# Local attention on row halves: scores and weighted values per head, on 64 rows and 32 columns of TensorE, in two parts

## The reference, cut to what matters

```
q, k, v = split(shift_tokens(x) @ Wqkv)            # to heads
q, k = rotate(l2norm(q) * q_scale), rotate(l2norm(k) * k_scale)
# every window of 32 queries sees the 64 keys of its own and the window before it
sim = einsum('bhwie,bhwje->bhwij', bq, bk2) * 8    # masked to a band
out = einsum('bhwij,bhwje->bhwie', softmax(sim), bv2)
x = out @ Wo + x
x = ffn_layer(shift_tokens(x)) + x                 # LayerNorm, W1, gelu gate, W2
```

## Time and profile before

| what | value |
|---|---|
| median of 3 runs | 6410.44 us (6407.3 to 6416.03) |
| the profiled execution | 6418.48 us, span 6416.7 us |
| PE, PEld busy | 5762.8 us (90%), 3834.2 us (60%) |
| DVE, ACT, POOL busy | 4902.8 us (76%), 3303.9 us (51%), 2795.0 us (44%) |
| L593 and L625, MATMUL | x12288 each, 274 ns each in the mean |
| mean granted clock of PE | 0.939 of full |
| HBM read, written | 36.20 MB, 1.05 MB |

### The profile page before, as it was taken

The page is one execution under the profiler, slowest core; times in us unless marked ns, Lnnn a source line. Parts: engine busy times, 40 slices in busy tenths (PEclk is TensorE's granted clock), DMA queues, the critical chain, the costliest instruction groups (busy, mean ns, idle before and its releaser), DMA issues. The chain is left out here.

```text
span 6416.7 us, 142352 instructions
## 1 busy us (share of the span) xinstructions
PE 5762.8 (90%) x47596; PEld 3834.2 (60%) x47596; DVE 4902.8 (76%) x9448; ACT 3303.9 (51%) x7050; POOL 2795.0 (44%) x3439
## 2 busy tenths in 40 slices
PE   4776999999999978988988998898699999999998
PEld 1334666666666644675566567457466666666665
DVE  5995776767676729998998999899577777677775
ACT  3334776777776732222222222223277777777775
POOL 1224666656666611222122123122266666666663
PEclk7998999999999988999999998999799999999998
DMA  0001222222222200000000000000022222222221
GB/s 16 0 0 53 67 74 71 67 66 67 73 64 73 65 22 0 1 1 1 0 1 1 1 1 1 1 1 1 23 68 73 65 74 64 75 68 70 68 67 41
DMA packets 163281, 247.28 MB, mean 39 GB/s; under 512 B 36980, under 2 KB 57392, under 8 KB 162486
## 3 DMA queue, kind: packets, MB, share of 16 engines
q1 hardware_dynamic: 162614, 238.71, 14.2%
HBM read 36.20 MB, written 1.05 MB: 6 GB/s over the span
## 5 line engine op out<-in xcount | busy, mean ns | idle before, releaser
L1428 PE MATMUL psum<-tk_kT,tk_qs 128*128 128x512 f32 (+3 forms) x4128 | 1255.7, 465 | 9.2 <-POOL tk_qs L1661 9.2
L1661 POOL TENSOR_TENSOR tk_qs<-tk_qT,tk_mix 128x1024 f32<-128x1024 f32 x258 | 495.7, 1924 | 1564.9 <-PE psum L1429 1441.8
L929 POOL TENSOR_TENSOR f_rope<-f_rope,f_t 128x1024 f32<-128x1024 f32 x384 | 905.5, 2358 | 476.7 <-DVE f_t L843 476.2
L1428 PEld LDWEIGHTS psum<-tk_kT,tk_qs 128*128 128x128 f32 x4128 | 757.0, 208 | 432.4 <-issue 290.2
L1618 DVE MAX8 tk_m<-tk_work 128x8 f32<-128x528 f32 (+3 forms) x1792 | 818.5, 496 | 2.2 <-issue 1.1
L942 POOL TENSOR_TENSOR f_rope<-f_rope,f_rn 128x1024 f32<-128x1024 f32 x384 | 730.5, 1902 | 59.9 <-POOL f_rn L921 4.4
L479 PE MATMUL psum<-f_wqkv,f_xs 128*128 128x512 f32 x1536 | 736.5, 602 | 16.7 <-DVE f_t L843 16.7
L1624 DVE MATCH_REPLACE8 tk_work<-tk_m,tk_work 128x400 f32<-128x400 f32 (+3 forms) x1536 | 744.0, 491 | 0.3
L848 DVE TENSOR_REDUCE f_ss<-f_sq 128x16 f32<-128x1024 f32 x384 | 466.0, 1213 | 339.3 <-ACT f_sq L710 334.6
L673 ACT ACTIVATE f_kT<-psum 64x512 f32<-64x512 f32 (+1 forms) x960 | 485.3, 525 | 82.5 <-PE psum L470 73.2
L1545 ACT ACTIVATE tk_o_tok<-psum,tk_rden 128x64 f32<-128x64 f32 (+1 forms) x256 | 80.0, 313 | 869.6 <-DVE tk_rden L1602 869.5
(11 more groups left out here) (235 smaller groups left out, 10226.4 us busy)
## 6 DMA issues: line engine op xcount, KB each, us to landing
f_v<-f_v_tok SPq DMA_DIRECT2D x1152, 128.0 KB, 2.4
f_v<-f_v_tok SPq DMA_DIRECT2D x768, 64.0 KB, 2.0
f_wqkv<-in_Wqkv SPq DMA_DIRECT2D x36, 512.0 KB, 5.2
f_wo<-in_Wo SPq DMA_DIRECT2D x12, 512.0 KB, 4.3
f_w<-in_W SPq DMA_DIRECT2D x12, 341.0 KB, 3.3
f_w<-in_W SPq DMA_DIRECT2D x24, 64.0 KB
tk_wkv<-in_Wkv SPq DMA_DIRECT2D x1, 1024.0 KB, 6.0
out<-y_tok SPq DMA_DIRECT2D x4, 256.0 KB, 2.5
```

What stands on the lines that cost most here:

```text
L929: pool.tensor_tensor(part, part, t2[:, half, :, :], ALU.add).then_inc(s[f"{name}_added"], 1)
L1428: pe.matmul(psum[:, j, 0:n], qs[:, j, c, :], kT[:, c, 0:n], start=(c == 0), stop=False, skip_group_check=True)
L1661: pool.tensor_tensor(qs[:, j, :, :], qT[:, :, P * t:P * (t + 1)], mix[:, :, heads(p, j)].to_broadcast([P, PAIRS, P]), ALU.mult).then_inc(s ...
```

## The change

Each head gets matmuls of its own on the 64 rows that hold it: 64 rows by 32 columns of weights, 64 moving columns. The zero blocks go: `kT` and `v2` lose the index `par`. The even heads' results go to bank 4, the odd heads' to bank 5, and VectorE reads and writes `o_tok` and `prob` by parity. `weigh` and `score` get an argument: part 0 makes pairs 0 to 3, part 1 pairs 4 to 7. `weigh(0)` stands ahead of `turn_keys` and `weigh(1)` behind it; `score(0)`, with the mask, stands behind `queries`, `score(1)` where `score` was. Part 0 waits only for the first bank's copies. ScalarE copies a bank's keys in one piece.

```diff
-        kT = sb("kT", [P, PAIRS, 2, WIN + 2 * P])
+        kT = sb("kT", [P, PAIRS, WIN + 2 * P])
-        v2 = sb("v2", [P, 2, WPT, 2, PAIRS, DH])
+        v2 = sb("v2", [P, 2, WPT, PAIRS, DH])
+        def by_parity(x):
+            return x.rearrange("p (c r) e -> p r c e", r=2)
...
-                            sp.dma_start(v2[r0:r0 + 2 * WIN, slot, w, par, :, :], v_tok[WIN * (w - 1):WIN * (w + 1), slot, par, :, :]).then_inc(v_in, 16)
+                            sp.dma_start(v2[r0:r0 + 2 * WIN, slot, w, :, :], v_tok[WIN * (w - 1):WIN * (w + 1), slot, par, :, :]).then_inc(v_in, 16)
...
-                    def weigh():
+                    def weigh(part):
                         if on(g, 2):
-                            for n in range(2):
-                                wait(pe, f"pt{n}_evac", through(g, 2))
-                            wait(pe, "sub_done", through(g, 2))
-                            pe.wait_ge(v_sem(j % 2), 1 + v_count(g - 2, j))
-                            for c in range(PAIRS):
+                            if part == 0:
+                                wait(pe, "sub_done", through(g, 2))
+                                pe.wait_ge(v_sem(j % 2), 1 + v_count(g - 2, j))
+                            wait_apart(pe, f"pt{part}_evac", through(g, 2))
+                            for c in range(4 * part, 4 * part + 4):
                                 for w in range(WPT):
-                                    last = pe.matmul(psum[WIN * w:WIN * (w + 1), 4 + c // 4, (c % 4) * P:(c % 4 + 1) * P],
-                                                     probT[:, c, WIN * w:WIN * (w + 1)], v2[:, j % 2, w, :, c, :], start=True, stop=True)
-                            last.then_inc(s["pv_done"], 1)
+                                    for par in range(2):
+                                        rows = slice(DH * par, DH * (par + 1))
+                                        last = pe.matmul(psum[WIN * w:WIN * (w + 1), 4 + par, c * DH:(c + 1) * DH],
+                                                         probT[rows, c, WIN * w:WIN * (w + 1)], v2[rows, j % 2, w, c, :], start=True, stop=True)
+                            if part:
+                                last.then_inc(s["pv_done"], 1)
...
-                    def score():
+                    def score(part):
                         if on(g, 1):
-                            for n in range(2):
-                                wait(pe, f"kt{n}_evac", through(g, 1))
-                                wait(pe, f"qt{n}_evac", through(g, 1))
-                            if on(g, 2):
-                                wait(pe, "on_done", through(g, 2))
                             sj = (j - 1) % 4
...
+                            wait(pe, f"kt{part}_evac", through(g, 1))
+                            if part == 0:
+                                if on(g, 2):
+                                    wait(pe, "on_done", through(g, 2))
+                                for par in range(2):
+                                    pe.matmul(psum[:, 4 + par, :], k.ident_bf[:, :], k.band[:, int(sj == 0), :, :].rearrange("p h w -> p (h w)"),
+                                              start=True, stop=False, skip_group_check=True)
+                            wait_apart(pe, f"qt{part}_evac", through(g, 1))
+                            for c in range(4 * part, 4 * part + 4):
...
+                                        last = pe.matmul(psum[WIN * w:WIN * (w + 1), 4 + par, c * 2 * WIN:(c + 1) * 2 * WIN],
+                                                         qT[rows, c, WIN * w:WIN * (w + 1)], kT[rows, c, t0:t0 + 2 * WIN],
+                                                         start=False, stop=True, skip_group_check=True)
...
+                    weigh(0)
                     turn_keys()
-                    weigh()
+                    weigh(1)
                     if f is not None and j == 2:
                         gated(1)
                     turn_queries()
                     queries()
+                    score(0)
                     if f is not None and j == 2:
                         gated(2)
-                        score()
+                        score(1)
                         output()
                     else:
                         output()
-                        score()
+                        score(1)
...
-                            for par in range(2):
-                                rows = slice(DH * par, DH * (par + 1))
-                                if sj == 1:
-                                    copy(kT[rows, 4 * n:4 * n + 4, par, 0:WIN], turned[rows, :, P - WIN:P])
-                                last = copy(kT[rows, 4 * n:4 * n + 4, par, slot:slot + P], turned[rows, :, :])
-                            last.then_inc(s[f"kt{n}_evac"], 1)
+                            if sj == 1:
+                                copy(kT[:, 4 * n:4 * n + 4, 0:WIN], turned[:, :, P - WIN:P])
+                            copy(kT[:, 4 * n:4 * n + 4, slot:slot + P], turned).then_inc(s[f"kt{n}_evac"], 1)
...
-                        dve.tensor_tensor(prob[:, :, :], sc_bank, top[:, :].unsqueeze(2).to_broadcast([P, H, 2 * WIN]), ALU.subtract).then_inc(s["sub_done"], 1)
+                        dve.tensor_tensor(by_parity(prob[:, :, :]), psum[:, 4:6, :].rearrange("p r (c w) -> p r c w", w=2 * WIN),
+                                          top[:, :].rearrange("p (r c) -> p r c", r=2).unsqueeze(3).to_broadcast([P, 2, PAIRS, 2 * WIN]),
+                                          ALU.subtract).then_inc(s["sub_done"], 1)
```

More of the change, by code:

```diff
@@ L426, in spread_v @@
                         r0 = DH * par
-                        sp.dma_start(v2[r0:r0 + WIN, slot, 0, par, :, :], v_tok[P - WIN:P, 1 - slot, par, :, :]).then_inc(v_in, 16)
-                        sp.dma_start(v2[r0 + WIN:r0 + 2 * WIN, slot, 0, par, :, :], v_tok[0:WIN, slot, par, :, :]).then_inc(v_in, 16)
+                        sp.dma_start(v2[r0:r0 + WIN, slot, 0, :, :], v_tok[P - WIN:P, 1 - slot, par, :, :]).then_inc(v_in, 16)
+                        sp.dma_start(v2[r0 + WIN:r0 + 2 * WIN, slot, 0, :, :], v_tok[0:WIN, slot, par, :, :]).then_inc(v_in, 16)
                         for w in range(1, WPT):
-                            sp.dma_start(v2[r0:r0 + 2 * WIN, slot, w, par, :, :], v_tok[WIN * (w - 1):WIN * (w + 1), slot, par, :, :]).then_inc(v_in, 16)
+                            sp.dma_start(v2[r0:r0 + 2 * WIN, slot, w, :, :], v_tok[WIN * (w - 1):WIN * (w + 1), slot, par, :, :]).then_inc(v_in, 16)
                 def layer(L):
@@ L609, in output @@
                             last.then_inc(s["wo_full"], 1)
-                    def score():
+                    def score(part):
                         if on(g, 1):
-                            for n in range(2):
-                                wait(pe, f"kt{n}_evac", through(g, 1))
-                                wait(pe, f"qt{n}_evac", through(g, 1))
-                            if on(g, 2):
-                                wait(pe, "on_done", through(g, 2))
-                            sj = (j - 1) % 4
-                            for half in range(2):
-                                pe.matmul(psum[:, 4 + half, :], k.ident_bf[:, :], k.band[:, int(sj == 0), :, :].rearrange("p h w -> p (h w)"),
-                                          start=True, stop=False, skip_group_check=True)
-                            for c in range(PAIRS):
+                            sj = (j - 1) % 4
+                            wait(pe, f"kt{part}_evac", through(g, 1))
[7 more added lines that the diff above has]
+                            for c in range(4 * part, 4 * part + 4):
@@ L623, in score @@
                                 for w in range(WPT):
                                     t0 = P * (sj % 2) + WIN * w
-                                    last = pe.matmul(psum[WIN * w:WIN * (w + 1), 4 + c // 4, (c % 4) * P:(c % 4 + 1) * P],
-                                                     qT[:, c, WIN * w:WIN * (w + 1)], kT[:, c, :, t0:t0 + 2 * WIN],
-                                                     start=False, stop=True, skip_group_check=True)
-                            last.then_inc(s["scores"], 1)
+                                    for par in range(2):
+                                        rows = slice(DH * par, DH * (par + 1))
+                                        last = pe.matmul(psum[WIN * w:WIN * (w + 1), 4 + par, c * 2 * WIN:(c + 1) * 2 * WIN],
+                                                         qT[rows, c, WIN * w:WIN * (w + 1)], kT[rows, c, t0:t0 + 2 * WIN],
+                                                         start=False, stop=True, skip_group_check=True)
@@ L630, in turn_output @@
+                            if part:
+                                last.then_inc(s["scores"], 1)
                     def turn_output():
@@ L815, in _ @@
             def _(dve):
-                dve.memset(kT[:, :, :, :], 0.0).then_inc(s["zeroed"], 1)
```

(7 more changed lines are left out.)

## The result

The changed kernel takes 6499.27 us in the median (6496.07 to 6502.99, 4 runs), beside 6409.9 for the kernel before in the same comparison: ratio 1.0138, 95% interval 1.0123 to 1.0153. It is slower by 1.4%; 6263 us had been forecast. No run of it came near the forecast range (6155 to 6397).

A forecast was written before the change was run, and what follows sets the result against it. TensorE's own work was taken to set the pace, with other limits close behind. Groups of four steps gave -151 us, memsets -10.8, jitter took back 14: -148 from 6418.5, less 8 for the profiled execution, 6263 us; range 6155 to 6397.

The forecast's parts named there:

- So issue is not what makes 27 ns today; the length of the moving rows is.: Matmul pricing: weight loads starting 7 ns apart were read as showing that moving-row length, not issue, sets 27 ns per record.
- Rival 3: All `weigh` and `score` matmuls: each costs 27 ns whatever its length, +3.86 us a step, ending at 7140; chance 5%.
- The visit, 8 x 0.054 + 0.23 = 0.66 us: One part of `weigh` or `score`: eight tiles at once, eight rounds plus fixed entry cost; 0.63 us saved per phase.
- rival 2: `weigh` and `score`: row halves don't overlap, each visit 1.09 us, +0.46 a step, ending at 6514, slower; chance 11%.
- P to Q 5.02, just above `k_rot`: From start of `turn_prob` (P) to start of `queries` (Q): 5.65 us becomes 5.02, still above `k_rot`'s 4.89 + 0.05.
- Q to P 10.06, bound by the chain: From `queries` to next `turn_prob`: 10.57 us becomes 10.06 at j=0, limited by projection, square, VectorE's work and exp.
- j=1 and SyncE's transfers: Step j=1: transfers into `v2`, 9.19 us behind `weigh`, hold `evacuate` and exp; step 15.14 us from 15.93, -0.79.
- rival 4: Other limits (j=2's delay, SyncE's transfers, two more entries) take 1 to 2.5 us per group, leaving 6310 to 6395; chance 13%.
- j=2, +0.34: Step j=2: `score(0)` ahead of `gated(2)` delays `hidden(2)`; `turn_prob` at 1746.61 against 1746.27, +0.34 us, less 0.63 ahead of `queries`.
- Memsets: Start of each stack: clearing `kT` and `v2`, 3.90 and 6.88 us, shrinks by half; 5.39 us each stack, -10.8.
- Copies of the keys, "nothing more": ScalarE's key copies, 2.42 us for four, 1.2 for two whole ones: saved copies are off the chain, gaining nothing more.
- The sum: Group of four steps: -3.15 us, over 48 groups -151; with memsets -10.8 and 14 set against jitter, -148.

The follow-up runs named there:

- e1_count: Kernel before, with every matmul of scores and weighted values cut into two of 64 moving columns on all 128 rows; 6553.7 us, ratio 1.0223.
- e8b_half: Row halves in both phases, one visit, order of before, each matmul 64 rows by 64 columns, 64 matmuls per visit as before; 6187.6 us, ratio 0.9647.
- e3_unsplit: Changed kernel with both parts of `weigh` and `score` one behind the other, in the order of before; 6466.5 us, ratio 1.0086.
- e11_burst: Kernel before, with matmuls that wait for nothing ahead of each stack's loop: 2048 of the changed form took 115.7 us, 1024 of the form before 61.46 us.
- e13_after_exp: Changed kernel with ScalarE's exponent put ahead of the copy of the values that waits for SyncE's transfers; 6448.7 us, ratio 1.0062.
- e4_gate_first: Changed kernel, but at j=2 `gated(2)` stands ahead of `score(0)` and `output` between the parts; 6457.3 us, ratio 1.0069.
- e2_order: Kernel before with its own matmuls, but `weigh` and `score` in two parts at the places of the changed kernel; 6641.0 us, ratio 1.0362.
- e5b_weigh_only: Kernel before with row halves in `weigh` only, `v2` without zeros, old order, scores and keys as before; 6448.7 us, ratio 1.0054.
- e6_score_only: Kernel before with row halves in `score` only, `kT` without zeros and copied whole, old order, `weigh` as before; 6385.2 us, ratio 0.9958.

## Why the prediction was wrong, point by point

- **The step that failed: "So issue is not what makes 27 ns today; the length of the moving rows is."** For a visit of before it holds: with shorter rows a matmul takes less there (e1_count, e8b_half). What failed is what was drawn from it, that after the change neither issue nor supply would bind, so that the visit was priced by columns alone. It was read from eight weight loads that start 7 ns apart. That is the pace of instructions already in hand, and not even that over a visit: 10.2 ns (e3_unsplit). Over a stretch the pace is the supply's, 27 ns for a matmul and its load (e11_burst), the same as four tiles of 128 columns need. Doubling the instructions to halve their length gains only as far as the blocks in hand reach. In the mean of the whole trace a part of `weigh` takes 0.95 us from its start to the next phase and a part of `score` 0.84, where 0.66 was forecast: 3.57 us a step instead of 2.64, which is 179 us over 192 steps if TensorE bounds them all (an estimate, which overlaps with the other points). About 100 us of it are the price of an unbroken visit, 0.79, the rest the breaks. Rival 3 had that price, and refuted itself on the earlier trace rows; it was right for a long stretch and wrong for a short one, which fits a result between the two.
- **The visit, 8 x 0.054 + 0.23 = 0.66 us**: row halves overlap, as said, and rival 2 falls. But the term was mis-sized: 0.79 for 64 matmuls, at 10.2 ns each instead of 6.7. The work between two parts holds TensorE longer too: `output` 1.98 us instead of 1.78. At j=0 P to Q gave 0.23 instead of 0.63, and Q to `turn_output` nothing (6.15 us after, from 1792.98 to 1799.13; before 6.13, from 1769.57 to 1775.70). The split itself was part of the price: e3_unsplit beats the changed kernel by 33 us.
- **P to Q 5.02, just above `k_rot`**: not reached at j=0 and j=1 inside the stacks; 5.41 and 5.44 at the least, 6.8 with a break.
- **Q to P 10.06, bound by the chain**: at j=0 TensorE is still the bound (10.60, with no idle). Where TensorE's work did shrink, in e8b_half, this step takes 15.09 us (1748.62 to 1763.71): P to Q 4.94, which is `k_rot`'s 4.89 and 0.05, and Q to P 10.15. The reading of the chain was right within 0.1 us, but the changed kernel doesn't get down to it.
- **j=1 and SyncE's transfers**: right that they come close, wrong in size. The breaks delay `weigh` and with it the transfers, and issues of up to 2 us, next to an instruction packet, are twice as many as before. This was rival 4's limit, and it holds the exponent at j=3 too; 51 us (e13_after_exp).
- **j=2, +0.34**: direction right. From Q to P it is 12.86 in the group shown (12.12 before), and taking the split away there gave 0.87 a group (e4_gate_first).
- **Memsets**: right. `kT` takes 1.98 us and `v2` 3.47, beside the 1.95 and 3.44 forecast.
- **Copies of the keys, "nothing more"**: half wrong. The forecast did see that the old ones would be late first behind `weigh`. They decide whether a shorter or later `weigh` pays (e2_order, e5b_weigh_only).
- **The sum**: against the forecast, the group shown lost 5.42 us: 1.80 at j=1 from P to Q (1.12 of it in the part that breaks, 1.91 us instead of 0.79), 1.21 in the other three such stretches, and 0.54, 0.81, 0.40 and 0.66 from Q to P. Over 48 groups that is 260 us, near the 236 that are missing and the 14 that were set aside for jitter; other groups have their breaks elsewhere.
- **Rival 4's range**: 2.5 us a group would end at 6383 by the forecast's own numbers, not 6395. Nothing hangs on it.

The chances had put 16% on slower, for reasons (rival 2, rival 3) that were not the one that came. No rival was a limit that shows only over a stretch; that is what was missing, and the Trainium skill, Advanced Engine Details and Errata, section ISA Cache, would have been the ground for one.

What stays open: in what way an instruction packet holds up an issue on SyncE, and whose packets do. Their number alone doesn't decide it: 379 packets and 87 long issues before, 475 and 91 in e6_score_only, 571 and 159 in e1_count, 571 and 197 after. Open too is how much of the 10.2 ns per matmul is the array and how much the sequencer.

## What to carry to other kernels

Count TensorE's instructions between two places as well as its columns: here a block of 256 (64 float32 products of two matmul records and two loads each) took 3.5 us or more from one to the next, and phases that used them up faster broke off, at places that moved when something was added ahead in the program. A finer tile paid where it caused hardly any breaks, as in the scores alone, -0.4%; halving the columns at the same number of matmuls gave 3.5% (e8b_half, which leaves out the right keys and values for every second window). And look at what stands behind a wait for a transfer on the same engine: exchanging two lines on ScalarE was worth as much as the scores' rework (another 0.4%), and together they make 6354.8 us of 6408.9.

## What the runs showed of the hardware that was not expected

- TensorE ran 448 instructions at first, then 256 at a time every 3.46 to 4.0 us at a granted clock of 0.50; at 1.00, once the stock was used up, 128 matmuls of the form of before took 3.7 us with their loads (1405 in 40.9 us).
- Every break of the changed kernel, 55 of 55, ended 1.2 to 1.6 us after the end of a 16 KB packet of the instruction queue.
- All issues of SyncE into `v2` of more than 1 us, 87 before and 197 after, overlapped such a packet; the usual one takes 0.5 to 0.6 us.
- 96 instructions that do nothing, ahead of the loop, moved the breaks to other steps and changed the time by 18 us (0.3%).
- Eight tiles of 64 rows and 32 columns took 10.2 ns for a matmul of 64 columns; four of 64 by 64 took 1.09 us for 64 matmuls, what the forecast's formula gives.
- Two visits of 64 matmuls with other work between cost 1.58 us, one of 128 costs 1.44; `output` between two visits took 0.20 longer than ahead of the band.
